# Row maximum of the attention scores: GpSimd's subtraction moved to VectorE, scores stored head-innermost

## The reference

```python
q, k, v = q.reshape(B, S, H, dh), k.reshape(B, S, H, dh), v.reshape(B, S, H, dh)
scores = jnp.einsum('bqhd,bkhd->bhqk', q * scale, k).astype(jnp.bfloat16)
probs = jax.nn.softmax(scores, axis=-1)
out = jnp.einsum('bhqk,bkhd->bqhd', probs.astype(jnp.float32), v)
h = h + out.astype(jnp.bfloat16).reshape(B, S, H * dh) @ Wo + bo
```

## Time and profile before

| | us |
|---|---|
| Median of 3 runs | 974.72 (974.15 to 976.13) |
| The profiled execution: its own time | 971.3 |
| Its span in the profile | 969.5 |
| Busy in that span: TensorE matmul | 699.7 |
| Busy: VectorE | 632.5 |
| Busy: ScalarE | 461.0 |
| Busy: GpSimd | 681.4 |

### The profile page before, as it was taken

The page is one execution under the profiler, slowest core; times in us unless marked ns, Lnnn a source line. Parts: engine busy times, 40 slices in busy tenths (PEclk is TensorE's granted clock), DMA queues, the critical chain, the costliest instruction groups (busy, mean ns, idle before and its releaser), DMA issues.

```text
span 969.5 us, 20598 instructions
## 1 busy us (share of the span) xinstructions
PE 699.7 (72%) x5680; PEld 582.5 (60%) x5680; DVE 632.5 (65%) x1723; ACT 461.0 (48%) x1091; POOL 681.4 (70%) x784
## 2 busy tenths in 40 slices
PE   4473499887997879878788787689877777776000
PEld 3362388776776768767677676458665655655000
DVE  1198478898999988999899788534333333333186
ACT  2021388776877867767677564114332323332000
POOL 4169444588787887878788778746777777777553
PEclk9686699999999999999999898589999999999555
DMA  8540000000000000000000000166665665663196
GB/s 200 157 136 22 12 1 2 9 26 28 19 27 19 22 29 17 27 22 22 27 17 24 20 24 27 40 184 200 202 183 170 178 183 168 176 186 111 50 347 215
DMA packets 71471, 85.57 MB, mean 88 GB/s; under 512 B 13943, under 2 KB 65152, under 8 KB 71355
## 3 DMA queue, kind: packets, MB, share of 16 engines
q1 hardware_dynamic: 33912, 37.34, 13.8%
q10 hardware_dynamic: 24976, 25.32, 9.3%
q0 software_dynamic: 12544, 22.44, 6.9%
HBM read 55.50 MB, written 31.85 MB: 90 GB/s over the span
## 4 chain that ended last, share of the span: by engine, by line
POOL 32%; issue 31%; PE 11%; DMA 6%; DVE 5%; POOLq 2%; ACT 1%; SPq 0%; DVEq 0%
POOL dispatched L528 11%; POOL expert_rows L541 8%; POOL s L483 7%; DMA x2t<-expert_rows 3%; POOL h L489 2%; DMA expert_rows<-yb,kz 2%; POOL rs L495 2%; PE bank L729 2%; PE bank L598 2%; PE bank L778 2%; DVE h L1258 1%; POOL ve L493 1%; PE bank L682 1%; PE bank L712 1%; PE bank L787 1%
## 5 line engine op out<-in xcount | busy, mean ns | idle before, releaser
L541 POOL DMA_INDIRECT expert_rows<-yb,kz x200 | 194.4, 972 | 75.4 <-issue 55.4
L528 POOL DMA_INDIRECT dispatched<-pay,sloti x192 | 198.7, 1035 | 60.9 <-issue 60.1
L483 POOL TENSOR_TENSOR s<-s,mx 113x904 bf16<-113x904 bf16 x64 | 109.4, 1709 | 49.9 <-DVE mx L1139 49.3
L1246 DVE TENSOR_TENSOR yb<-bank,kz 128x256 f32<-128x256 f32 x100 | 42.4, 424 | 142.8 <-DMA expert_rows<-yb,kz 139.2
L729 PE MATMUL bank<-kz,qt 128*113 128x226 f32 x512 | 112.1, 363 | 0.3 <-ACT kz L859 0.3
L778 PE MATMUL bank<-xe,w_ex 128*128 128x256 f32 x400 | 105.8, 388 | 0.0
L917 ACT ACTIVATE xe<-bank 128x256 f32<-128x256 f32 x100 | 38.3, 383 | 139.7 <-PE bank L766 132.1
L598 PE MATMUL bank<-xt,wqkv 128*128 128x452 f32 x384 | 103.2, 400 | 0.9 <-DVE xt L1157 0.7
L787 PE MATMUL bank<-w_ex,hide 128*128 128x128 f32 x400 | 67.6, 292 | 48.6 <-DVE hide L1236 46.4
L787 PEld LDWEIGHTS bank<-w_ex,hide 128*128 128x128 f32 x400 | 55.5, 192 | 75.1 <-DVE hide L1236 58.8
L729 PEld LDWEIGHTS bank<-kz,qt 128*113 128x113 f32 x512 | 89.6, 185 | 6.8 <-issue 0.7
(11 more groups left out here) (161 smaller groups left out, 1705.9 us busy)
## 6 DMA issues: line engine op xcount, KB each, us to landing
w_ex<-in_w_ffn ACTq DMA_DIRECT2D x100, 192.0 KB, 2.5
kz<-dispatched SPq DMA_DIRECT2D x100, 130.0 KB, 2.4
x2t<-expert_rows SPq DMA_DIRECT2D x16, 672.0 KB
x2t<-in_x SPq DMA_DIRECT2D x8, 864.0 KB, 6.0
out_h<-h ACTq DMA_DIRECT2D x16, 224.0 KB
expert_rows<-yb,kz POOLq DMA_INDIRECT x200, 2.5
dispatched<-pay,sloti POOLq DMA_INDIRECT x192, 2.3
h<-in_txt SPq DMA_DIRECT2D x1, 2464.0 KB
```

What stands on the lines that cost most here:

```text
L483: nc.gpsimd.tensor_tensor(s16[k % 2][0:T, :, :], s16[k % 2][0:T, :, :], mx[k % 2][0:T, :].unsqueeze(2).to_broadcast([T, H, T]), ALU.subtra ...
L528: pool.indirect_dma_start(out=xs_dram[:, :], out_offset=bass.IndirectOffsetOnAxis(ap=sloti[:, b // GRP, b % GRP, c:c + 1], axis=0), in_=pa ...
L541: pool.indirect_dma_start(out=y_dram[:, :], out_offset=bass.IndirectOffsetOnAxis(ap=xs[slot][:, j, ROW - 1:ROW].bitcast(I32), axis=0), in_ ...
```

## The change

The score buffer becomes [query, key, head]. ScalarE's two copies write four heads each into it, so that neighbouring elements of what they write lie 8 elements (16 bytes) apart; VectorE's maximum over keys and ScalarE's exponential read it at the same pitch. The subtraction leaves GpSimd's stream and stands in VectorE's, right behind the maximum, for which it waits. There its two inputs and its output run along memory with the 8 heads innermost. The probabilities keep their layout.

```diff
-        s16 = [sb(f"s16_{i}", [128, H, T], BF16) for i in range(2)]
+        s16 = [sb(f"s16_{i}", [128, T, H], BF16) for i in range(2)]
...
-                if ok(n):
-                    after(pool, "max_done", n)
-                    nc.gpsimd.tensor_tensor(s16[k % 2][0:T, :, :], s16[k % 2][0:T, :, :],
-                                            mx[k % 2][0:T, :].unsqueeze(2).to_broadcast([T, H, T]), ALU.subtract).then_inc(S["sub_done"], 1)
...
-                    nc.scalar.activation(p16[k % 2][0:T, :, :], s16[k % 2][0:T, :, :], ACT.Exp).then_inc(S["exp_done"], 1)
+                    nc.scalar.activation(p16[k % 2][0:T, :, :], s16[k % 2][0:T, :, :].rearrange("p t h -> p h t"), ACT.Exp).then_inc(S["exp_done"], 1)
...
-                        m = nc.scalar.activation(s16[(k + 1) % 2][0:T, 4 * i:4 * i + 4, :].rearrange("p h t -> p (h t)"),
-                                                 bank[3 + i][0:T, 0:4 * T], ACT.Copy)
+                        m = nc.scalar.activation(s16[(k + 1) % 2][0:T, :, 4 * i:4 * i + 4].rearrange("p t h -> p h t"),
+                                                 bank[3 + i][0:T, 0:4 * T].rearrange("p (h t) -> p h t", t=T), ACT.Copy)
...
-                    nc.vector.reduce_max(mx[i][0:T, :], s16[i][0:T, :, :], AX.X).then_inc(S["max_done"], 1)
+                    nc.vector.reduce_max(mx[i][0:T, :], s16[i][0:T, :, :].rearrange("p t h -> p h t"), AX.X).then_inc(S["max_done"], 1)
+                    after_all(dve, ("txt_in", 16), ("max_done", n, 1))
+                    nc.vector.tensor_tensor(s16[i][0:T, :, :], s16[i][0:T, :, :],
+                                            mx[i][0:T, :].unsqueeze(1).to_broadcast([T, T, H]), ALU.subtract).then_inc(S["sub_done"], 1)
```

## The result

The changed kernel takes 1277.9 us (median of 4 runs, 1276.8 to 1281.2) where the kernel before takes 974.7: 1.313 times as long, 95% interval 1.308 to 1.318. The forecast was 959.3 with a range up to 1022. It fell on the wrong side, and even the slow rival was far too small.

What follows compares the result with a forecast made beforehand. The prediction took GpSimd to bound the attention loop, stalling VectorE. Saving 17 us in the loop and 2 at the end, losing 3.6 at the start, made -15.4: 959.3 us, own range 948 to 970, all cases 948 to 1022.

Steps and rivals of the forecast that it cites:

- the slow rival: The pitch costs: VectorE's maximum takes 0.94 us more, 64 times; 1019 us, 1050 possible if ScalarE doubles; chance 0.24.
- What bounds the kernel: Attention loop: GpSimd is the bound, and its subtraction stalls VectorE by 6.5 us in eight steps.
- The subtraction at 0.62 us: On VectorE, two bf16 elements a cycle: 0.62 us, adding 0.72 a step, or 1.19 at the upper bound.
- The maximum at a pitch: VectorE's maximum reading at 16 bytes: no added time, upper bound 0.94 us more.
- ScalarE at a pitch: Exponential and two score copies unchanged; upper bound some 0.75 us more for the exponential and 0.75 for both copies.
- the ring: Round from maximum through subtraction, probabilities copy, residual add, value products, scores and score copies to next maximum; not in the prediction.
- ScalarE has cover: Loop: ScalarE is busy 46.1 of 61.7 us, with 7.6 of its idle time spent waiting for GpSimd's subtraction.
- the sum: Whole kernel: -17 in the loop, +3.6 at the start, -2 at the end, together -15.4 us.
- octet: Eight loop steps: 59.2 us in place of 61.7, saving 2.5, or 17 us over 55 steps.
- The first eight steps: Start of attention, paced by TensorE: a loss of 0.45 us a step, 3.6 us.
- the remainder: End of attention, behind the last maximum, closing with a row of GpSimd sends: a gain of 2 us.
- The rival in which VectorE gives nothing back: VectorE becomes the bound and its waits for GpSimd's power, 2.3 us in eight steps, stay: 975 us; chance 0.10.

Runs made afterwards that it cites:

- all dense: Changed kernel (also called "everything dense") with score copies, maximum and exponential all side by side, subtraction still head-innermost on VectorE: 943.1 us, ratio 0.970.
- 8 bytes: Changed kernel with four heads innermost, so neighbours in the stream lie 8 bytes apart: 1004.3 us, ratio 1.030.
- pairs: Changed kernel with two heads innermost, a 4-byte pitch: 948.8 us; rerun 949.9 us, and 944.2 us with copies in output order on the same chip.
- dense writes: Changed kernel with only ScalarE's two score copies written side by side again, maximum and exponential still reading at 16 bytes: 1009.2 us, ratio 1.038.
- Move only: Kernel before, its old score layout kept, with the subtraction moved from GpSimd to VectorE: 976.2 us, ratio 1.003.
- the write's order: Changed kernel, same layout, with the score copies written in memory order and the pitch moved to the PSUM read: ratio 1.038.

## Why the prediction was wrong

**What bounds the kernel: right.** GpSimd was the bound of the loop, and its subtraction blocked VectorE. In the version with everything dense L1182 and L1020 no longer have their long stalls, and the loop is 31 us shorter though VectorE has an instruction more. How much of that is GpSimd's load and how much the blocking was not separated.

**The subtraction at 0.62 us: right**, 0.63, and 1.10 in the old layout, the upper bound of 1.09.

**The maximum at a pitch, taken at zero: wrong.** It measured +0.70 us, inside its bounds (0 to 0.94). The row on which it leaned, L1046 of the earlier trace rows, has a pitch of 64 bytes over three elements and comes back to the same three lines. The text said so, and still took it for the new pattern. The Trainium skill's rule on lines ("Advanced Engine Details and Errata", SBUF Cachelines) gave the right sign: at 16 bytes every read pays. It gave no size. By the Trainium skill's same section at least two hits on a line are needed to absorb the latency. At 8 bytes, two to a line, that fits the maximum (1094 ns for 1087) and nearly the exponential (1034 for 958), but not the write (1241 for 545).

**ScalarE at a pitch, taken as unchanged: wrong, and this is the step that failed.** "Bounds: the same, or an element doubled" had no row behind the upper end at all. The exponential, a read, stayed near it (+0.88 against 0.75). The two copies, writes, took 3.7 us more in a step against a bound of 0.75 for both: nearly five times. As they overlap a little, 3.2 of it is on the ring. The range was too narrow because the bound for an unknown write was borrowed from a guess about reads.

**"ScalarE has cover": wrong.** Its idle time was counted, not its place. The copies stand on the ring from one maximum to the next, which in the first stretch was already as long as a step, 6.06 us, and in the loop had some 1.7 us of room below the step of 7.73. Once that room is used up, whatever is added to the ring is added to the step, however idle ScalarE is. The smaller pitches show the room: 0.28 us more in the two copies (pairs, with and without the write in order) cost 5.7 us over all 64 steps, not 18, but 1.4 us more (8 bytes, against all dense) cost 1.0 us in each step of the loop, 8.18 for 7.16.

**The slow rival had the right place but the wrong line.** It priced the maximum and left the copies as a remark, 1019 to 1050 us. For the case that it did price it was near: dense writes, where only the reads have the pitch, measured 1009. Its threshold, the maximum 0.25 us longer, was crossed by 0.70.

**The clock was not in the sum.** The ring grew by 1.5 us through score matmuls at the lower clock. The clock fell together with TensorE's long waits: in all dense, without them, the loop had 0.99. That the waits are the cause is likely, but no run shows it by itself.

**The sum itself, without the pitch, was too high.** All dense measured 943.1, not 959.3. By its terms: the loop's 55 steps lost 31.1 us (424.9 to 393.8) where 17 were taken. An octet there takes 57.3 us, not 59.2: VectorE busy 53.6, where the sum had 54.8, and idle 3.7, where it had 4.4. The first eight steps cost 2.0, not 3.6; the remainder gave 1.5, not 2. Move only shows the same surplus (976 for 989): the terms leaned to the slow side together, so even without the pitch the forecast would have lain some 14 us too high on one and the same chip. The rival in which VectorE gives nothing back is refuted by the same run.

## What to carry to other kernels

When a layout changes, ask for each engine that touches it in which order it now reads and in which order it now writes; let the pitch fall on a side that is measured to bear it, here the read from PSUM. Two elements side by side were enough for VectorE's higher rate, so a small inner group can do what a full transposition did. And before an engine's idle time is used as cover, follow the ring of queues on which the instruction stands: once the ring is as long as the step, each microsecond on it counts once per step.

## What the runs showed of the hardware

ScalarE's copy of 452 scores from PSUM into bf16 took 545 ns at a write pitch of 2 bytes, 687 at 4, 1241 at 8 and 2367 at 16. From 4 bytes on, each further byte of pitch costs 0.31 ns an element (1241 less 687 over 452 elements and 4 bytes, and 2367 less 1241 over 8); from 2 to 4 bytes it is half of that. The distance covered on average is not what counts: with four elements side by side and 8 bytes left out behind them (the write's order) a copy takes 552 ns, though it moves 4 bytes along for each element like the copy of 687. Reads are cheaper: ScalarE's exponential of 904 elements took 958, 960, 1034 and 1838 ns at the same pitches, and VectorE's maximum 1087, 1094, 1094 and 1784. From side by side to 16 bytes that is 0.97 and 0.77 ns more an element, against 4.03 for the write. The runs don't show what in the write makes it four times as dear as the read, nor how other types behave.
